# A third batch's best keys searched at the end of the causal attention, and the local attention's second half of the first norm on ScalarE

## The chip, the cores and the metric

The program runs on one core of a Trainium2 chip. The metric is the device time of one execution of the whole program in microseconds (us). A kernel stands with the median of its runs. Beside them one execution was taken by the hardware profiler; all times of engines below are from it, counted from the start of its span. In its views PE is TensorE, PEld its weight loads, DVE VectorE, ACT ScalarE, POOL GpSimd, SP SyncE, which issues the transfers.

## The reference, cut to what matters

Twelve layers follow each other, each `x = x + layer(norm(x))`, with x of 8 batches of 128 tokens and 128 features. The change touches three layers in a row.

- `L1_attn`, causal attention with 16 heads of width 64: softmax(q k / scale) v, projected.
- `L1_xattn`, attention to a context in which each query keeps only its 32 best keys: 4 heads of width 32; per row of 128 scores the 32 largest are kept, the rest is left out of the softmax. Its probabilities, averaged over the heads, weigh the context's values; a product with `film` gives scales and shifts (FiLM) for the layer's inputs, which are x normed twice, times `g_norm_in` plus `b_norm_in`. A long convolution along the tokens (a state space model) and a two-layer MLP follow.
- `L1_ffn`, two small blocks, each a local attention with l2-normed, rotated queries and keys (8 heads of width 64) and a gated MLP.

## The kernel before, in words

Every layer is one or two blocks. In a block each engine has a list of instructions of its own, run in order; semaphores (`wait_ge`, `then_inc`) tie the lists, and at a block's end all engines meet. Next to nothing is planned at run time: the order is the order of the loops.

**Causal attention (`layer_l1_attn`).** The loop runs over turns -6 to 16; turn n holds step n of 16 (half a batch, 8 heads), and in it TensorE turns the probabilities of step n (L2339), makes the scores of step n+2 (L2375, L2379) and the value products of step n (L2395); ScalarE takes the exponentials of step n+1 (L2463) and copies step n's result (L2490); VectorE copies turned probabilities (L2556), inverts sums (L2561) and takes maxima of step n+2 (L2602); GpSimd divides the probabilities of step n+1 (L2253). In turns 4, 8, 14 and 16 two finished batches are projected (L2353) and GpSimd adds them to x (L2267). In between, work of the next layer is fitted in: the keys, queries and scores of batches 0 and 1, and `ROUNDS` says in which turn how many rounds of `BestKeys.one_round` VectorE runs. A round takes the eight largest of each row (`max`, L2122) and takes them out (`match_replace`, L2129) for four heads; four rounds make a batch. In turn 14 x's batches 2 and 3 are measured for the norm, in turn 16 they are normed (L2526), turned (L2303), copied, and their queries made (L2401); in turns 15 and 16 the keys of batches 2 to 7 are made (L2297); the scores of batch 2 close TensorE's list (L4023, L4026).

**Best keys (`top_attention`), called the top stage below.** VectorE finishes the norm's statistics and searches batches 2 to 7, four rounds each, with the norm of batches 4 to 7 (`dve_xn`, L464) after the second round. ScalarE copies scores out (L4251), takes the exponentials of a batch's scores (L4240, `exps`) and of what the search left (L4230, `exps_left`), and empties the banks of means (L4257), context (L4261) and FiLM (L4219, L4221). GpSimd subtracts the two (L4115), makes the weight from the two sums (L4104 to L4106) and multiplies (L4118, which marks `kept`), later modulates the inputs (L4123, L4127) and adds x to the shifts (L4130). In its turn 3 it begins the inputs of all 8 batches (L4096 to L4099). TensorE turns the kept probabilities (L4184), multiplies with the values (L4193) and with `film` (L4197, L4201), and makes the scores of a batch two turns on. `keep_clock_bf` (L134) gives it products that nobody reads: 8 before the loop, 6 and 5 near its end, 4 behind it. SyncE first issues the next layer's weights (3698 KB, L4776), then stores the convolution's taps to DRAM (L4071), waits for them and reads them back as rows (8 transfers of 1024 KB, L4077) for the next block, `state_space_out`, whose convolution (L4358) needs all of them.

**Local attention (`layer_l1_ffn`).** GpSimd takes the root of the second half's variance (L482, `norm.pool(pool, 1)`), makes tables (L3334), rotates (L3345, L3347) and takes powers (L3378). VectorE norms batches 4 to 7 (`norm.dve_xn(dve, 1)`, L464, four instructions), then sums squares of batch 2 (L3769), which ScalarE has squared (L3601). TensorE turns the normed batches (L488); the copies of them (L3594 by ScalarE, L3701 by VectorE) stand before the first value products (L3500).

## Time and the profile before

| | us |
|---|---|
| median of 3 runs (lowest, highest) | 1181.59 (1180.98, 1185.31) |
| the profiled execution, its own time | 1178.47 |
| its span, first to last instruction | 1176.7 |
| top stage, from its first instruction on VectorE to the first product of the convolution | 362.23 to 421.55 |

Over the whole span TensorE is busy 91%, VectorE 57%, ScalarE 47%, GpSimd 39%; these are means over stages with different limits. In a timeline a row gives the start, the duration, the engine, the line and operation, and in brackets how long the engine stood idle before it and which instruction ended that. The granted TensorE clock is given as a share of 2.4 GHz: 0.50 is its lower level, 1.2 GHz.

### The profile page before, as it was taken

How to read it: one execution, taken by the hardware profiler on the slowest of the kernel's cores; microseconds unless marked ns; L12 is line 12 of the kernel's file. 1: busy time of each engine (PE TensorE's matmuls, PEld its weight loads, DVE VectorE, ACT ScalarE, POOL GpSimd, SP SyncE). 2: the span in 40 equal slices, each digit the busy share in tenths (PEclk: the TensorE clock that was granted, in tenths of full speed). 3: DMA queues.
4: the chain of work that ended last, by engine and by line, in shares of the span. 5: the costliest groups of instructions: out<-in, count | busy, mean ns of one | idle time of the engine just before them, and what ended most of it. 6: DMA issues, size and time to landing. Idle time of an engine off the chain costs nothing. (4 is left out here: it accounts for less than half of the span.)

```text
span 1176.7 us, 22941 instructions
## 1 busy us (share of the span) xinstructions
PE 1065.6 (91%) x8781; PEld 765.7 (65%) x8797; DVE 673.5 (57%) x2055; ACT 557.6 (47%) x1473; POOL 461.4 (39%) x545
## 2 busy tenths in 40 slices
PE   6999989899997689898999899978899999988996
PEld 5876858567674355676677566745567776666684
DVE  5555562445767846885678467638823117766512
ACT  5434334266575844355445455506543334653432
POOL 7968913123245943783487250012000004041423
PEclk9999999899998799999999999999999999999999
DMA  5000060232205801000000030000021100010312
GB/s 168 1 1 5 2 232 1 94 105 73 73 2 205 216 2 46 1 1 1 1 2 1 1 76 2 2 5 33 1 81 36 36 19 17 2 41 2 130 48 77
DMA packets 55084, 54.18 MB, mean 46 GB/s; under 512 B 19472, under 2 KB 45840, under 8 KB 53952
## 3 DMA queue, kind: packets, MB, share of 16 engines
q1 hardware_dynamic: 54048, 50.84, 14.0%
q0 software_dynamic: 928, 1.88, 0.5%
q8 instruction: 71, 1.16, 0.4%
q14 instruction: 37, 0.30, 0.1%
HBM read 44.08 MB, written 8.63 MB: 45 GB/s over the span
## 5 line engine op out<-in xcount | busy, mean ns | idle before, releaser
L482 POOL TENSOR_TENSOR ln_rstd<-ln_ve,ln_half 128x4 f32<-128x4 f32 x25 | 25.4, 1018 | 251.7 <-DVE ln_ve L457 251.7
L652 DVE TENSOR_REDUCE scratch<-bank 128x4 f32<-128x512 f32 x96 | 63.3, 684 | 31.2 <-PE bank L557 18.1
L1311 ACT ACTIVATE scratch<-bank 128x512 f32<-128x512 f32 x64 | 38.2, 596 | 66.2 <-PE bank L1267 66.2
L713 ACT ACTIVATE scratch<-bank 128x512 f32<-128x512 f32 x96 | 55.5, 597 | 23.4 <-PE bank L572 23.0
L2253 POOL TENSOR_TENSOR scratch<-scratch 128x512 f32<-128x512 f32 x32 | 33.3, 1040 | 82.7 <-DVE scratch L2561 82.6
L1330 DVE SCALAR_TENSOR_TENSOR x_res<-bank,scratch,x_res 128x128 f32<-128x128 f32 x64 | 18.0, 344 | 82.1 <-PE bank L1277 82.1
L1277 PEld LDWEIGHTS bank<-weights,scratch 128*128 128x128 f32 x512 | 59.5, 192 | 7.2 <-issue 7.2
L572 PE MATMUL bank<-ident,scratch 128*128 128x128 f32 x384 | 56.8, 278 | 7.9 <-ACT scratch L707 6.0
L3378 POOL TENSOR_TENSOR scratch<-scratch 128x16 f32<-128x16 f32 x16 | 50.6, 3163 | 33.4 <-DVE scratch L3774 24.9
L1267 PE MATMUL bank<-xnT,weights 128*128 128x512 f32 x128 | 59.2, 606 | 0.7 <-ACT xnT L1300 0.7
L1277 PE MATMUL bank<-weights,scratch 128*128 128x128 f32 x512 | 59.6, 275 | 0.0
L572 PEld LDWEIGHTS bank<-ident,scratch 128*128 128x128 f32 x384 | 42.6, 141 | 20.3 <-ACT scratch L707 8.4
L659 DVE TENSOR_TENSOR scratch<-bank,scratch 128x512 f32<-128x512 f32 x72 | 47.2, 683 | 0.8
L2463 ACT ACTIVATE scratch<-bank,scratch 128x128 f32<-128x128 f32 x128 | 45.0, 386 | 4.1 <-DVE scratch L2602 4.0
L3994 POOL TENSOR_TENSOR scratch<-scratch 128x1024 f32<-128x1024 f32 (+5 forms) x48 | 42.9, 894 | 3.8
L3989 POOL TENSOR_TENSOR scratch<-scratch 128x2048 f32<-128x2048 f32 x8 | 36.2, 4524 | 17.3 <-DVE weights L1870 16.9
L1267 PEld LDWEIGHTS bank<-xnT,weights 128*128 128x128 f32 x128 | 23.7, 196 | 24.7 <-issue 23.8
L1595 ACT ACTIVATE scratch<-bank 128x512 f32<-128x512 f32 (+1 forms) x44 | 22.7, 524 | 34.9 <-PE bank L1507 33.6
L3601 ACT ACTIVATE scratch<-bank 128x512 f32<-128x512 f32 x32 | 19.2, 599 | 40.4 <-PE bank L3415 40.4
L3036 POOL TENSOR_TENSOR scratch<-weights,xnT 128x128 f32<-128x128 f32 x8 | 3.4, 428 | 84.9 <-DVE weights L3252 84.9
L134 PE MATMUL bank<-key_bias,ident_bf 128*128 128x512 bf16 x115 | 33.9, 412 | 2.4 <-ACT weights L4275 1.1
L3415 PE MATMUL bank<-weights,xnT 128*128 128x512 f32 x64 | 31.8, 616 | 3.5 <-DVE scratch L3707 1.6
(645 smaller groups left out, 2913.7 us busy)
## 6 DMA issues: line engine op xcount, KB each, us to landing
scratch<-conv_kernels SPq DMA_DIRECT2D x8, 1024.0 KB, 11.2
weights<-e_l_ffn_w SPq DMA_DIRECT2D x20, 256.0 KB, 2.9
scratch<-e_l_ffn_w SPq DMA_DIRECT2D x4, 1024.0 KB, 15.2
values<-scratch SPq DMA_DIRECT2D x8, 512.0 KB, 2.7
scratch<-values SPq DMA_DIRECT2D x8, 512.0 KB, 4.3
weights<-w_l_ffn SPq DMA_DIRECT2D x1, 3698.0 KB, 11.6
scratch<-e_l_ffn_w SPq DMA_DIRECT2D x4, 768.0 KB, 6.9
weights<-w_l_attn SPq DMA_DIRECT2D x1, 2560.5 KB, 9.2
```

What stands on the lines that cost most here:

```text
L134: self.nc.tensor.matmul(self.ps[bank][:, :], self.ident_bf[:, :], self.key_bias[:, 0:BANK], start=True, stop=True)
L572: t = self.nc.tensor.transpose(self.core.ps[4 + n % 2][:, i * P:(i + 1) * P], self.shift[:, n % 4, i * P:(i + 1) * P], self.core.ident[:, :])
L652: self.nc.vector.tensor_reduce(self.top[:, n % 4, :], self.by_head(self.core.ps[n % 4][:, :]), AX_X, ALU.max, negate=True).then_inc(self.t ...
L659: self.nc.vector.tensor_tensor(self.by_head(self.shift[:, n % 4, :]), self.by_head(self.core.ps[n % 4][:, :]), self.top[:, n % 4, :].unsqu ...
L713: self.nc.scalar.activation(self.prob_of(n), self.by_head(self.core.ps[4 + n % 2][:, :]), ACT.Exp, scale=scale) \
L1267: nc.tensor.matmul(ps[UP_BANKS[i]][:, :], wa[e % 2][:, i * P:(i + 1) * P], core.xnT[:, half(h)], start=True, stop=True).then_inc(up_made.s ...
L1277: mm = nc.tensor.matmul(ps[Y_BANKS[u % 3]][:, t * P:(t + 1) * P], hT[h][:, i, t * P:(t + 1) * P], wb[e % 2][:, i, :], start=(i == 0), stop ...
L1311: nc.scalar.activation(hT[u % 2][:, i, :], ps[UP_BANKS[i]][:, :], act_func) \
L2463: a = nc.scalar.activation(prob[:, r, 4 * i + j, :], score_bank(n + 1, i)[:, j * P:(j + 1) * P], ACT.Exp, bias=top[:, r, 4 * i + j:4 * i + ...
L3378: nc.gpsimd.tensor_tensor(rn_first[:, s + 2, :] if s + 2 < FIRST else rn, ss, power, ALU.pow) \
L3989: link(tt(prod, z, wa[:, a].unsqueeze(1).broadcast_to([P, R, 2 * N]), ALU.mult))
L3994: link(tt(out, prod[:, :, 0:h], prod[:, :, h:2 * h], ALU.add))
```

## The change

It does six things.

1. Batches 2 and 3 of x are measured in turn 9, rooted and normed in turn 10, turned and copied in turn 11; their keys are made in turn 12 and their queries in turn 13. TensorE's products for it go to the bank of the step before, and VectorE, not ScalarE, empties them.
2. In turn 15 the scores of batch 2 (`score_third`) take the place of the keys' product; they lie in two banks and ScalarE copies them out. VectorE searches batch 2 in turn 16, four rounds (`STEPS: (4,)`). The scores of batch 3 close TensorE's list. ScalarE takes both exponentials of batch 0 in turn 16.
3. The inputs' first half (batches 0 to 3) is begun by GpSimd in turn 15 (`begin_inputs(..., 0)`), the second half in turn 3 of the top stage.
4. The top stage searches batches 3 to 7; the norm of batches 4 to 7 follows the first round; scores are made three turns ahead. Of the products nobody reads, the 8 before the loop and the 5 before the last batch's turning go, and 6 become 3.
5. The taps are stored at the end of SyncE's list in the causal attention. In the top stage SyncE reads the rows first and issues the next layer's weights behind them.
6. In the local attention GpSimd makes the offsets -mean times root (`pool_centred`), and ScalarE norms batches 4 to 7 with them (`act_xn`) in front of squaring batch 2; VectorE's four instructions go.

```diff
+    def pool_centred(self, pool, h, offset, centred):
+        core, nc, rows = self.core, self.nc, slice(B // 2 * h, B // 2 * (h + 1))
+        pool.wait_ge(self.eps.sem, self.half(self.eps, h))
+        nc.gpsimd.tensor_scalar(offset, core.ln_mv[:, rows, 0], -1.0, None, ALU.mult).then_inc(centred.sem, centred.up())
+        self.pool(pool, h)
+        pool.wait_ge(self.rstd.sem, self.half(self.rstd, h))
+        pool.wait_ge(centred.sem, centred.at(0))
+        nc.gpsimd.tensor_tensor(offset, offset, core.ln_rstd[:, rows], ALU.mult).then_inc(centred.sem, centred.up())
+
+    def act_xn(self, act, h, offset, centred):
+        act.wait_ge(centred.sem, centred.at(1))
+        for b in range(B // 2 * h, B // 2 * (h + 1)):
+            n = b - B // 2 * h
+            self.nc.scalar.activation(self.out[:, b, :], self.src[:, b, :], ACT.Identity, bias=offset[:, n:n + 1],
+                                      scale=self.core.ln_rstd[:, b:b + 1]).then_inc(self.xn.sem, self.xn.up())
...
+def begin_inputs(core, link, pool, search, u, g_in, b_in, h):
+    rows = slice(B // 2 * h, B // 2 * (h + 1))
...
+    link(tt(var, core.ln_mv[:, rows, 1], core.ln_rstd[:, rows], ALU.mult))
+    link(tt(var, var, core.ln_rstd[:, rows], ALU.mult))
+    link(ts(var, var, 1e-5, None, ALU.add))
+    link(tt(rstd, var, core.ln_half[:, rows], ALU.pow))
+    link(tt(part, core.xn[:, rows, :], rstd.unsqueeze(2).broadcast_to([P, B // 2, D]), ALU.mult))
+    link(tt(part, part, every(g_in), ALU.mult))
+    link(tt(part, part, every(b_in), ALU.add))
...
-    ROUNDS = {6: (0, 0, 0, 1), 7: (0, 0, 2, 0), 8: (2, 0, 1, 0), STEPS - 2: (0, 0, 2, 0)}
+    ROUNDS = {6: (0, 0, 0, 1), 7: (0, 0, 2, 0), 8: (2, 0, 1, 0), STEPS - 2: (0, 0, 2, 0),
+              STEPS: (4,)}
...
+            sp.dma_start(core.conv_dram.ap(), core.conv_kp).then_inc(taps.sem, taps.up(16))
+            sp.wait_ge(taps.sem, taps.at(0, 16))
...
+                if n == STEPS - 1:
+                    pool.wait_ge(*core.w_loaded["l1_xattn"])
+                    pool.wait_ge(ahead.rstd.sem, ahead.half(ahead.rstd, 0))
+                    pool.wait_ge(ahead.xn.sem, ahead.batch(ahead.xn, 3))
+                    pool.wait_ge(filled.sem, filled.at(place["yT", 2, 1]))
+                    begin_inputs(core, link, pool, search, inputs_at, g_in, b_in, 0)
...
+            def prepare_second_pair(n, out):
+                if n == 11:
+                    turn_rows(out, 2).then_inc(ahead.turned.sem, ahead.turned.up())
+                if n == 12:
+                    next_keys(0, out)
+                if n == 13:
+                    pe.wait_ge(x_out.sem, x_out.at(2))
+                    nc.tensor.matmul(out[:, 0:2 * P], wq_next, core.xnT[:, 2 * P:4 * P], start=True, stop=True) \
+                        .then_inc(queries_made.sem, queries_made.up())
...
                 if n == STEPS - 1:
-                    next_keys(0)
+                    pe.wait_ge(keys_out.sem, keys_out.at(0))
+                    pe.wait_ge(queries_out.sem, queries_out.at(0))
+                    score_third()
                 if n == STEPS:
-                    next_keys(1)
-                    pe.wait_ge(copied.sem, copied.at(2 * STEPS - 1))
-                    turn_rows(ps[T_BANKS[0]], 2).then_inc(ahead.turned.sem, ahead.turned.up())
+                    pe.wait_ge(third_copied.sem, third_copied.at(0))
+                    next_keys(1, ps[S_BANKS[1]])
+                if n in (11, 12, 13):
+                    pe.wait_ge(outs.sem, outs.at(n - 1))
+                    prepare_second_pair(n, ps[O_BANKS[(n - 1) % 2]])
...
             for t in range(1, B + 2):
-                if t == FIRST + 1:
-                    begin_inputs()
+                if t == 1:
+                    norm.pool(pool, 1)
+                if t == 3:
+                    norm.wait_xn(pool, B - 1)
+                    pool.wait_ge(norm.rstd.sem, norm.half(norm.rstd, 1))
+                    begin_inputs(core, link, pool, search, u, g_in, b_in, 1)
...
-            core.keep_clock_bf(QUERY_BANK, 8)
+            score(4)
...
-                if b == LAST:
-                    core.keep_clock_bf(SCORE_BANKS[3], 5)
...
-                    core.keep_clock_bf(SCORE_BANKS[3], 6)
+                    core.keep_clock_bf(SCORE_BANKS[3], 3)
...
+            core.load_following(sp)
...
-                        norm.pool(pool, 1)
+                        norm.pool_centred(pool, 1, norm_offset, norm_centred)
...
+                    if s == 0 and d == 0:
+                        norm.act_xn(act, 1, norm_offset, norm_centred)
                     if s + 2 < B:
                         square(g + 2)
...
                     if s == 0 and d == 0:
-                        norm.dve_xn(dve, 1)
                         sum_squares(g + 2)
```

## Rows read from the trace of the kernel before

**Rows 1.** The page: its first line, the span.

```profile
span 1176.7 us, 22941 instructions
```

**Rows 2.** Timeline: start, us, engine, line, operation, [idle before <-releaser]. A causal turn.

```profile
341.50 0.66 PE L2339 MATMUL bank<-ident,scratch 128*128 128x128 f32 x4 [0.51 <-POOL scratch L2253]
...
344.75 0.58 ACT L2490 COPY scratch<-bank 128x512 f32<-128x512 f32 x1 [0.91 <-PE bank L2395]
```

**Rows 3.** Timeline, last two turns of the causal attention and the stage change.

```profile
351.75 0.60 PE L2297 MATMUL bank<-ctxT_sb,weights 96*128 96x256 f32 x2
...
355.28 0.38 PE L2303 MATMUL bank<-ident,xn 128*128 128x128 f32 x2
...
359.37 0.70 PE L2401 MATMUL bank<-xnT,weights 128*128 128x256 f32 x2
...
359.47 0.62 ACT L2474 ACTIVATE scratch<-bank,weights 128x128 f32<-128x128 f32 x2 [3.13 <-PE bank L2353]
...
361.07 0.72 POOL L2267 TENSOR_TENSOR x_res<-x_res,scratch 128x256 f32<-128x256 f32 x1 [8.03 <-ACT scratch L2497]
...
362.23 0.49 DVE L444 BATCH_NORM_STATS2 ln_st<-x_res 128x6 f32<-128x128 f32 x2 [7.94 <-PEq L2226]
```

**Rows 4.** VectorE in the top stage: the norm, two starts of a search.

```profile
366.75 1.11 DVE L464 TENSOR_SCALAR xn<-x_res,ln_mv,ln_rstd 128x128 f32<-128x128 f32 x4
...
386.22 0.86 DVE L2122 MAX8 scratch<-weights 128x8 f32<-128x128 f32 x4
...
393.54 0.86 DVE L2122 MAX8 scratch<-weights 128x8 f32<-128x128 f32 x4
```

**Rows 5.** Groups in 362 to 422: xcount | busy us, mean ns | idle.

```profile
L4240 ACT ACTIVATE scratch<-weights 128x128 f32<-128x128 f32 x32 | 12.4, 394 | 0.0
```

**Rows 6.** Timeline of GpSimd in the top stage.

```profile
377.93 1.04 POOL L4096 TENSOR_TENSOR scratch<-xn,scratch 128x512 f32<-128x512 f32 x1
...
384.84 1.27 POOL L4115 TENSOR_TENSOR scratch<-scratch 128x512 f32<-128x512 f32 x1
...
387.47 0.27 POOL L4106 TENSOR_SCALAR scratch<-scratch,text_on 128x4 f32<-128x4 f32 x1
...
388.82 0.46 POOL L4123 TENSOR_TENSOR scratch<-scratch,weights 128x128 f32<-128x128 f32 x1
...
390.24 1.27 POOL L4115 TENSOR_TENSOR scratch<-scratch 128x512 f32<-128x512 f32 x1
...
410.66 0.46 POOL L4123 TENSOR_TENSOR scratch<-scratch,weights 128x128 f32<-128x128 f32 x1
```

**Rows 7.** TensorE, the top stage's last batches and the next stage.

```profile
401.49 0.80 PE L4193 MATMUL bank<-scratch 128*128 128x128 f32 x2 [0.36 <-ACT scratch L4257]
403.18 2.08 PE L4197 MATMUL bank<-weights,scratch 128*128 128x512 f32 x2 [0.90 <-ACT scratch L4261]
...
414.34 2.34 PE L134 MATMUL bank<-key_bias,ident_bf 128*128 128x512 bf16 x5
...
421.55 1.95 PE L4358 MATMUL bank<-scratch 128*8 128x128 f32 x64 [1.19 <-PEq L4067]
...
434.49 0.38 DVE L4475 TENSOR_TENSOR scratch<-bank,scratch 128x128 f32<-128x128 f32 x1
```

**Rows 8.** A stretch: us, busy time by engine, PEclk, DMA share, GB/s.

```profile
402.00:406.00 4.00, 3.10 (x8) 1.25 (x7) 4.00 (x28) 3.88 (x19) 3.60 (x7) 0.50 0.65 164
```

**Rows 9.** Timeline of SyncE's queue at the start of the top stage.

```profile
374.15 24.66 SPq L4077 DMA_DIRECT2D scratch<-conv_kernels  x8
```

**Rows 10.** Timeline at the first batches of the local attention.

```profile
471.35 1.01 POOL L482 TENSOR_TENSOR ln_rstd<-ln_ve,ln_half 128x4 f32<-128x4 f32 x1 [0.55 <-DVE ln_ve L457]
...
479.55 2.90 POOL L3378 TENSOR_TENSOR scratch<-scratch 128x16 f32<-128x16 f32 x1 [1.75 <-DVE scratch L3774]
...
474.77 3.37 DVE L464 TENSOR_SCALAR scratch<-x_res,ln_mv,ln_rstd 128x128 f32<-128x128 f32 x4
...
480.49 1.87 PE L3500 MATMUL bank<-scratch 128*128 128x65 f32 x12 [1.97 <-DVE xnT L3701]
```

## What the change should do to the time

> **What bounds the kernel now.** I read the page's first line for the size of the whole [rows 1] and then the timelines of the three stages that the change touches, since a mean over 1176.7 us says nothing of them. In each the question is which wait ends last.
>
> In the causal attention's late turns the work of a step goes from engine to engine in a ring: GpSimd divides, TensorE turns, VectorE copies, TensorE multiplies, ScalarE copies out and takes the next exponentials. TensorE waits for GpSimd (0.51 us) and ScalarE for TensorE (0.91 us) in the same turn [rows 2]: no engine is full, the ring itself is the limit, and what is put into it may lengthen it. At the stage's end the picture is another one. VectorE has nothing from 354.29 to 362.23 (7.94 us), ScalarE stands still for 3.13 us before the last projection arrives, and GpSimd's last addition, at 361.07, ends the stage [rows 3].
>
> In the top stage VectorE is never idle: a batch's search takes 393.54 - 386.22 = 7.32 us, and it does six [rows 4]. That looks like the bound, but it is not what ends the stage. GpSimd begins the inputs at 377.93 and takes batch 2 only at 384.84, 6.91 us later; from then on it takes one batch every 5.40 us with hardly a gap, up to the sixth's kept probabilities at 410.66 [rows 6]. TensorE's film product for that batch waits for them, five unread products follow at 414.34 (2.34 us), then the last batch, and the convolution starts at 421.55 [rows 7]. GpSimd's list ends last, the search a little before it.
>
> In the local attention four norm instructions take VectorE 3.37 us [rows 10], 0.84 each, where four of the same shape take 1.11 in all in the top stage [rows 4]; the sum of squares, GpSimd's power at 479.55 (1.75 us idle) and TensorE's value products at 480.49 (1.97 us idle) wait behind them [rows 10].
>
> **Causal attention, turns 9 to 14.** TensorE gets 0.38 (turning two batches), 0.60 (keys) and 0.70 us (queries) [rows 3], 1.68 us in turns 11 to 13, all of it between the turning and the value products, so in the ring. VectorE gets a norm of two batches (half of 1.11, 0.56 us [rows 4]), statistics (at most the same again) and three copies out of banks of 256 columns (0.38 to 0.60 each by the nearest rows [rows 3], 1.5 us at 0.5): 2.6 us. The copies of VectorE fall where TensorE is still busy with scores, and half of TensorE's extra falls into the waits for GpSimd (0.51 every second turn). Taken along the ring turn by turn, about 1.0 us stays. Bounds: 0 if the waits take all, 1.68 + 2.6 = 4.3 if nothing hides. The new waits of TensorE (for a step's copy out by ScalarE) come after the turning (341.50 in the turn shown [rows 2]), when the copy of the step before is past; behind them stand the scores, for which VectorE and ScalarE wait.
>
> **Causal attention, the end.** The search of batch 2 is 7.32 us of VectorE. Its cover is the idle 7.94 us plus the 0.56 of norm that leaves turn 16: 8.5 us, and the scores have to be there in time; they are, for they come where the keys' product stood (351.75) [rows 3] and VectorE is free only at about 353.7. So VectorE ends at about 361, beside GpSimd's last addition. Cost 0, margin about 1 us; without the cover, 7.3. ScalarE's eight exponentials, 394 ns each [rows 5], are 3.15 us in an idle time of 3.13 [rows 3]; the 256-column copy that leaves makes room. GpSimd's first half of the inputs (3.46 of big instructions, some 1.8 of small ones) lies in its 8.03 us of idleness [rows 3]. The turning (0.38) and part of the queries' product (0.70) leave the chain to the end: -0.4. The taps' transfer stands last in SyncE's list, behind transfers that are long done. Causal attention in all: +0.6, bounds -0.4 and +3.9.
>
> **Top stage.** VectorE loses one search of six, 7.32 us. GpSimd: batch 0's exponentials are ready, so it starts right after the root, at about 364.1, and is done 3.98 later (388.82 - 384.84 [rows 6]). Batch 1 needs its second exponentials, behind the copy of the turned norm; the norm now comes one round (1.83) earlier: 0.8 statistics, 1.83, 1.11 norm [rows 4], 1.1 turning, 0.6 copy and 4 x 0.394 [rows 5] after 362.2 give 369.2. Then 3.98 for batch 1, 1.8 for small instructions (four, nearest rows 0.27 and 1.01 [rows 6, 10]) and 6.91/2 = 3.46 for half the inputs: batch 2 starts at 378.5, not 384.84 [rows 6]. From there the pace is the old 5.40, since each batch costs what it cost: **-6.3 us**. The search does not hold it up: five searches and the norm end at 401, and the last batch's exponentials of what is left, at 404, come before GpSimd's last kept probabilities (410.66 - 6.3 = 404.4).
>
> The five unread products (2.34 us [rows 7]) stood between the sixth batch's film product and the last batch's turning; about 0.2 of it lay beside other work: **-2.1 us**. The eight and the three others stood in waits: 0. So -8.4 at an unchanged clock.
>
> The clock is not unchanged. From 402 to 406 it was granted at 0.50, the lower level [rows 8], though TensorE was busy 3.10 of 4 us; the film product took 2.08 us there and the values' product 0.80 [rows 7]. It is at 2.4 GHz when the convolution starts: 64 products in 1.95 us [rows 7]. Ahead of that stood the five unread products. With 16 such products gone the last two batches' products can take twice what they take at the higher level (half of 2.08, of 0.80 and of a turning like the latter, 1.9 a batch), +3.8, and the convolution's first 64 another 1.95: between 0 and +5.7. I take +2.0, since part of the last batches ran at the lower level before, too.
>
> The Trainium skill, "TensorE: Matmul & The Clock Gate", Part 1, says that the default state is throttled and that activity releases the throttle; that speaks against taking unread products out. The trace agrees as far as a lower level stands in the stretch with gaps. By it, in full, the stage would give the 5.7 and end near -2.7; by the rows of unread products alone it would be -8.4.
>
> The transfers: the eight row reads are issued from 374.15 on, over 24.66 us [rows 9], and the queues are still busy in part of 402 to 406 [rows 8], so they end near 404. They now start near 362.6 and end near 393; the next weights follow and are needed only behind 458. Cost 0; the rows would matter only if they came after 413. In all -6.4, bounds -8.4 and -2.7.
>
> **Local attention.** VectorE loses 3.37 us. GpSimd gets two small instructions (0.27 at most each [rows 6]) and two waits: its tables and rotation come 0.9 later. ScalarE gets four instructions of some 0.4 us (394 ns [rows 5]), 1.6 us, in front of squaring batch 2, which is late by as much; the power on GpSimd then starts at 478.65, when the rotation is over, not 479.55: -0.9. The normed batches are turned and copied at about 478.0, so the value products start 2.4 us before 480.49 [rows 10]. Which of the two counts? The next powers wait for TensorE's chain, with more idle time than 0.9 in front of them, so -2.2; bounds -0.9 and -2.5.
>
> **Sum.** +0.6 - 6.4 - 2.2 = -8.0. The profiled execution took 1178.47 (span 1176.7 [rows 1], 1.8 around it); it would become 1170.5. The median of the runs shown is 1181.59, 3.1 above it, so I predict 1173.6.
>
> **Rivals.** (a) The ring is lengthened by everything that is put in: +3.9 in place of +0.6, so -4.7, 1176.9. For it: no engine in it has slack in every turn [rows 2]; against: the waits of 0.51 and 0.91. (b) The clock stays low through the last batches and the convolution's start, +5.7 in place of +2.0: -4.3, 1177.3. (c) The clock does not fall: -10.0, 1171.6. (d) Slower: TensorE stays at 1.2 GHz through the whole convolution. That stage is 12.9 us (421.55 to 434.49 [rows 7]) and ordered by TensorE; doubled it adds 12.9, with 3.8 for the two batches 16.7 in place of 2.0: +6.7, 1188.3. It decides from 8.0 us of clock loss beyond my 2.0. Against it: the convolution is dense, 64 products in 1.95 us. (e) The change doesn't do what it says: the third search is not hidden but ends the stage. If the scores come late or the rounds slow down beside GpSimd, up to 7.3 - 1.0 = 6.3 of the gain is handed back: -1.7, 1179.9. Against it is the 8.5 us of cover [rows 3].
>
> **Chances.** Forecast, with all its terms near their values: 0.50. (a) 0.14, (b) 0.12, (c) 0.12, (d) 0.06, (e) 0.06. Half a per cent, 5.9 us, is about what a measurement can tell. The forecast's own range, 1171 to 1176, is beyond it in nine parts of ten: 0.45; with (c) and what of (a) and (b) ends beyond it, 0.63 faster; 0.30 the same; 0.07 slower. The range runs from the sum of the good bounds, -0.4 - 8.4 - 2.5 = -11.3, 1170.3 (1169.5 with a little for the median), to (e), 1180.
>
> **What would show it.** Right: VectorE searching up to the end of the causal attention and that stage no more than 2 us longer; GpSimd taking batch 2 some 16 us after the top stage's start and then every 5.4 us; the convolution starting 53 us after the stage's start, not 59.3; the four norms on ScalarE at about 0.4 us, value products about 2 us sooner. Wrong: a PE clock near 0.5 in the convolution; an idle VectorE in the top stage, waiting for scores of batch 4; a top stage in which ScalarE, not GpSimd, ends last; turns 10 to 13 more than 0.5 us longer each.

## The result: faster by 1.0%, more than forecast

| | before | after |
|---|---|---|
| median (lowest, highest), us | 1181.28 (1179.90, 1185.31) | 1169.22 (1168.38, 1170.57) |
| the profiled execution, us | 1178.47 | 1170.57 |
| its span, us | 1176.7 | 1168.8 |

The ratio is 0.990, with a 95% interval of 0.988 to 0.992, which is 10.0 to 14.4 us less. Forecast was 1173.6 with a range of 1169.5 to 1180.0: the direction was right, the gain a third too small, and the measured median 0.3 us below the range. Two later series of the same two kernels gave ratios of 0.991 (0.989 to 0.994) and 0.990 (0.988 to 0.991), so 10 to 12 us is the size to explain, and that the first median lies 0.3 us below the range is within what the series differ by.

Where it is, by stages of the two profiled executions (starts by SyncE's first transfer of a stage or VectorE's first statistics, ends by the next stage's start; the top stage ends with the convolution's first product):

| stage | before | after | difference | forecast |
|---|---|---|---|---|
| stage ahead of the causal attention (unchanged code) | 63.07 | 66.01 | +2.9 | 0 |
| causal attention | 142.64 | 143.27 | +0.6 | +0.6 |
| top stage | 59.32 | 51.34 | -8.0 | -6.4 |
| convolution and MLP | 36.56 | 36.57 | 0 | 0 |
| local attention | 221.58 | 218.42 | -3.2 | -2.2 |
| all behind it | 491.81 | 492.14 | +0.3 | 0 |

The three changed stages give -10.5 us. The +2.9 in unchanged code is no effect of the change: the same stage took 63.07 us in two other executions of changed kernels (again_2 and norm_back below) and 65.7 to 66.1 in most others. It goes with the granted clock, whose mean over this stage was 0.97 in the execution of before, 0.92 in that of after, 0.93 in "again" (65.77 us) and 1.00 in both_early (62.83 us).

The top stage after, GpSimd's timeline (start, duration, engine, line and operation, and in brackets how long the engine was idle and what ended that). These answer to [rows 6]; the subtraction is L4204 now, the modulation L4212:

```profile
381.76 1.10 POOL L4204 TENSOR_TENSOR scratch<-weights,scratch 128x512 f32<-128x512 f32 x1
...
387.00 1.27 POOL L4204 TENSOR_TENSOR scratch<-scratch 128x512 f32<-128x512 f32 x1
...
406.98 0.47 POOL L4212 TENSOR_TENSOR scratch<-scratch,weights 128x128 f32<-128x128 f32 x1
```

The reader is to see the starts of the large subtractions. The stage starts at 365.56; batch 2 (381.76) is taken 16.2 us later, where the forecast had 16.3 and the kernel before 22.6, and from there the starts are 5.24, 5.42, 5.33 and 5.42 apart. The kept probabilities of batch 6, the last that GpSimd makes (the prediction calls it the sixth), are done at 407.0, 41.5 us after the start instead of 48.5. The durations of L4204 alternate between 1.09 or 1.10 and 1.27; before, all seven took 1.27.

TensorE at the end of the stage, answering to [rows 7]:

```profile
408.93 1.81 PE L4281 MATMUL bank<-weights,scratch 128*128 128x512 f32 x2 [0.35 <-ACT scratch L4345]
...
410.96 1.06 PE L4268 MATMUL bank<-ident,scratch 128*128 128x128 f32 x4
...
416.90 1.95 PE L4441 MATMUL bank<-scratch 128*8 128x128 f32 x64 [1.57 <-PEq L4168]
```

and the granted clock there (a stretch, its length, TensorE's busy time and instructions, PEclk, DMA share, GB/s), answering to [rows 8]:

```profile
404.00:408.00 4.00, 2.17 (x7) 1.00 0.06 24
...
410.00:412.00 2.00, 2.00 (x7) 0.50 0.00 0
...
414.00:418.00 4.00, 2.43 (x48) 1.00 0.01 2
```

From 404 to 408 the clock is 1.00, from 410 to 412 it is 0.50, and the film product (1.81 us) and the turning (1.06) are drawn out there; ahead of the convolution it is back at 1.00. From 404 on the transfers have all but ended (24 GB/s), and TensorE waits for none.

The causal attention's end, answering to [rows 3]:

```profile
357.19 0.85 DVE L2156 MAX8 scratch<-weights 128x8 f32<-128x128 f32 x4
...
365.60 0.49 DVE L444 BATCH_NORM_STATS2 ln_st<-x_res 128x6 f32<-128x128 f32 x2 [1.01 <-PEq L2265]
...
364.43 0.73 POOL L2315 TENSOR_TENSOR x_res<-x_res,scratch 128x256 f32<-128x256 f32 x1 [3.18 <-ACT scratch L2580]
```

VectorE searches from 357.19 to 364.6 where it stood idle for 7.94 us; the next stage's statistics come 1.01 us after that, and GpSimd's last addition ends at 365.16, 0.6 us after the search. The search is hidden.

The turns with the extra work, before and after: ScalarE copies out the results of steps 10, 11 and 12 (the first step is 0):

```profile
332.28 0.58 ACT L2490 COPY scratch<-bank 128x512 f32<-128x512 f32 x1 [0.18 <-PE bank L2395]
...
336.73 0.58 ACT L2490 COPY scratch<-bank 128x512 f32<-128x512 f32 x1 [0.91 <-PE bank L2395]
...
340.45 0.58 ACT L2490 COPY scratch<-bank 128x512 f32<-128x512 f32 x1 [0.33 <-PE bank L2395]
```

```profile
335.09 0.59 ACT L2573 COPY scratch<-bank 128x512 f32<-128x512 f32 x1 [0.17 <-PE bank L2476]
...
339.79 0.59 ACT L2573 COPY scratch<-bank 128x512 f32<-128x512 f32 x1 [1.14 <-PE bank L2476]
...
343.95 0.59 ACT L2573 COPY scratch<-bank 128x512 f32<-128x512 f32 x1 [0.77 <-PE bank L2476]
```

They were 4.45 and 3.72 us apart and are 4.70 and 4.16: 0.69 us more, and every other distance between the copies is the old one within 0.02 us. From the last copy to the next stage it takes 7.62 us instead of 7.80.

The local attention, answering to [rows 10]:

```profile
468.30 1.65 ACT L482 ACTIVATE scratch<-x_res,scratch,ln_rstd 128x128 f32<-128x128 f32 x4 [5.15 <-POOL scratch L476]
...
473.66 1.97 PE L3601 MATMUL bank<-scratch 128*128 128x65 f32 x16 [1.36 <-DVE xnT L3804]
475.47 1.04 PE L3532 MATMUL bank<-ident,scratch 128*128 128x128 f32 x8
```

The four norms take ScalarE 0.41 us each. The value products start 20.2 us after the stage's start (453.47), before 22.4 (480.49 - 458.11): 2.2 sooner. They and the turning behind them take 1.97 and 1.04 us; before, they took 2.72 and 1.91, with the clock at its lower level. The row in [rows 10] gives 1.87 us and 12 products because its view ended at 482; all 16 are here:

```profile
480.49 2.72 PE L3500 MATMUL bank<-scratch 128*128 128x65 f32 x16 [1.97 <-DVE xnT L3701]
483.01 1.91 PE L3431 MATMUL bank<-ident,scratch 128*128 128x128 f32 x8
```

```profile
482.00:484.00 2.00, 2.00 (x11) 2.00 (x11) 1.51 (x5) 0.00 (x0) 1.20 (x2) 0.50 0.00 0
```

In this last view of before each engine has a busy time, TensorE first; the granted clock is the third number from the end. GpSimd's power starts 20.2 us after the stage's start, before 21.4: 1.3 sooner (forecast 0.9).

### The profile page after: what moved, and what is told of

Same layout as the page of the kernel before. It is cut to its first block and busy times, and to the rows that moved or that the text cites. A ratio compares the mean times of both kernels' runs of the same rounds, so it can differ in the third digit from the quotient of the medians.

```text
span 1168.8 us, 22936 instructions
## 1 busy us (share of the span) xinstructions
PE 1063.2 (91%) x8781; PEld 762.9 (65%) x8781; DVE 671.9 (57%) x2054; ACT 559.2 (48%) x1475; POOL 463.3 (40%) x551
## 3 DMA queue, kind: packets, MB, share of 16 engines
q0 software_dynamic: 928, 1.88, 0.5%
## 5 line engine op out<-in xcount | busy, mean ns | idle before, releaser
L2338 PE MATMUL bank<-xnT,weights 128*64 128x128 f32 x512 | 32.4, 277 | 2.6 <-DVE scratch L2660 1.0
## 6 DMA issues: line engine op xcount, KB each, us to landing
weights<-w_l_ffn SPq DMA_DIRECT2D x1, 3698.0 KB, 16.2
```

## Experiments

All kernels start from the changed one unless it says otherwise. The series ran on more than one chip (the kernel before took 1181 us in two of them and 1188 to 1190 in the others); a ratio is always to the kernel before of the same series, and stage lengths come from the profiled execution of each. "Kept" is the end of batch 6's kept probabilities, the last that GpSimd makes, counted from the stage's start.

| kernel | ratio (95% interval) | causal | kept | top stage | local |
|---|---|---|---|---|---|
| before | 1 | 142.64 | 48.5 | 59.32 | 221.58 |
| after, first | 0.990 (0.988, 0.992) | 143.27 | 41.5 | 51.34 | 218.42 |
| again | 0.991 (0.989, 0.994) | 142.79 | 41.5 | 50.69 | 218.40 |
| again_2 | 0.990 (0.988, 0.991) | 143.10 | 41.4 | 51.27 | 218.38 |
| norm_back | 0.994 (0.992, 0.996) | 143.10 | 41.4 | 51.30 | 221.28 |
| norm_keep | 0.990 (0.989, 0.992) | 141.79 | 42.9 | 52.07 | 219.90 |
| norm_alone (from before) | 0.999 (0.997, 1.000) | 142.49 | 48.5 | 58.97 | 218.59 |
| five_back | 0.991 (0.989, 0.993) | 142.84 | 41.5 | 51.26 | 218.39 |
| keepers_all | 0.994 (0.992, 0.996) | 142.66 | 44.2 | 55.45 | 218.36 |
| e_placed | 0.990 (0.988, 0.992) | 143.14 | 41.2 | 51.53 | 218.38 |
| halves_late | 0.995 (0.994, 0.997) | 142.81 | 47.0 | 56.25 | 219.14 |
| rounds_four | one run | 142.98 | 48.1 | 57.59 | 218.38 |
| rounds_late | one run | 142.74 | 42.8 | 56.76 | 219.16 |
| norm_later | one run | 142.65 | 44.4 | 54.30 | 218.36 |
| end_more | one run | 142.78 | 42.9 | 52.48 | 218.56 |
| no_adds | one run | 142.71 | 40.5 | 50.30 | 218.39 |
| left_first | 0.992 (0.991, 0.994) | 143.22 | 43.5 | 52.91 | 218.38 |
| left_placed | 0.992 (0.990, 0.993) | 142.90 | 43.6 | 52.81 | 219.15 |
| mean_early | 0.991 (0.989, 0.993) | 142.71 | 42.5 | 51.69 | 219.14 |
| both_early | 0.990 (0.988, 0.992) | 141.69 | 42.2 | 51.45 | 218.39 |

**The change again (again, again_2).**

> The changed kernel once more. The three changed stages of its first profile sum to 10.5 us less than before (0.7 more in the causal attention, 8.0 less in the top stage, 3.2 less in the local attention). If that is the whole change, five rounds give 10.0 to 11.2 us below the kernel before; if the first medians' difference of 12.1 us is real, something outside these stages gives 1.5 us.

> The changed kernel on this chip, for comparison with the two below, and a third measurement of the change itself: 10.0 to 11.2 us below before if the three stages are all of it; 12 if the first measurement's median was right.

The kernel was 10.6 and 11.8 us below before. The three changed stages account for 10.0 to 11.7, by three executions of the changed kernel and two with the old code in the first two stages (before, and norm_alone). Nothing outside them is needed, and nothing outside them is seen; 10.6 is what was expected of the three stages alone, and the 11.8 of again_2 lies between its two values, 10.0 to 11.2 and 12.

**The local attention's edit undone (norm_back).**

> The changed kernel with the local attention's norm as before: VectorE norms batches 4 to 7, GpSimd makes no offsets. By the prediction's term the kernel is 2.2 us slower than the changed one and its value products keep TensorE's full clock. By the rival, a fall of the clock after TensorE's idle time of about 2 us costs another 1.0: 3.2 us slower, with a slice at 0.50 and value products of 2.7 us instead of 2.0 in this stage.

```diff
-                        norm.pool_centred(pool, 1, norm_offset, norm_centred)
+                        norm.pool(pool, 1)
...
-                    if s == 0 and d == 0:
-                        norm.act_xn(act, 1, norm_offset, norm_centred)
...
                     if s == 0 and d == 0:
+                        norm.dve_xn(dve, 1)
                         sum_squares(g + 2)
```

The median is 3.1 us above the same chip's "again", the stage 2.9 longer. TensorE of this kernel and its granted clock:

```profile
472.91 2.07 PE L3601 MATMUL bank<-scratch 128*128 128x65 f32 x16 [1.94 <-DVE xnT L3802]
474.78 1.91 PE L3532 MATMUL bank<-ident,scratch 128*128 128x128 f32 x8
```

```profile
474.56:476.56 2.00, 2.00 (x12) 0.52 0.00 0
```

TensorE is idle for 1.94 us, starts its value products 22.35 us after the stage's start, and the clock falls behind that, to 0.52 and in the next slice 0.63: the turning takes 1.91 us where after it takes 1.04. So here the edit is worth 3 us, not 2.2, and a fall of the clock follows the idle time. The edit makes the fall rarer and does not rule it out: in 4 of the 17 executions with the edit the clock fell at this place all the same (halves_late, rounds_late, left_placed, mean_early). The idle time ahead is 1.34 to 1.38 us in all 17, and the local attention of the four took 219.14 to 219.16 us instead of 218.4 to 218.6. One slice of halves_late, 22 us into the stage:

```profile
478.50:480.50 2.00, 2.00 (x11) 0.51 0.00 0
```

**The idle time filled (norm_keep).**

> The changed kernel with the local attention's norm as before (VectorE norms batches 4 to 7) and seven products that nobody reads between the turning of the normed batches and the first value products, where TensorE stood idle for 1.94 us. If the edit's gain of 3.0 us was 2.0 to 2.2 from the earlier start and about 1.0 from a clock that did not fall, the local attention takes about 220.3 us here (221.3 without the seven products, 218.4 in the changed kernel) and the value products take 1.04 us instead of 2.07. If the clock has no part in it, it stays at 221.3.

```diff
                         turn_x(d, 1)
+                        core.keep_clock_bf(O_BANKS[0], 7)
```

```profile
474.63 1.97 PE L3601 MATMUL bank<-scratch 128*128 128x65 f32 x16
476.44 1.04 PE L3532 MATMUL bank<-ident,scratch 128*128 128x128 f32 x8
```

```profile
474.43:476.43 2.00, 1.97 (x17) 1.00 0.00 0
```

The value products start at the same place (22.2 us after the stage's start), the clock stays at 1.00, the turning takes 1.04 and the stage 219.90 instead of 221.28. So of the edit's 2.9 us, 1.4 are the clock that doesn't fall and 1.5 the earlier start, when the fall is taken away first. Taken the other way, between executions that both show the fall (norm_back and halves_late, 221.28 and 219.14), the earlier start is worth 2.1 and the fall 0.8. One number of the expectation missed: the value products themselves took 1.97 against 2.07, not 1.04; it is the products behind them that doubled. The medians of norm_back and norm_keep lie further apart (0.994 and 0.990) than the stage explains, and no other stage shows the rest. Norm_keep's top stage, with the code of the changed kernel, took 52.07 us and its kept probabilities came at 42.9: the granted clock was at its lower level from about a microsecond after the stage's start (see end_more below).

**That edit alone, on the kernel before (norm_alone).**

> The kernel before with the local attention's edit alone (offsets by GpSimd, the second half of the norm by ScalarE). If the edit's worth doesn't hang on the rest: about 3.0 us faster than before, its local attention 218.4 us long. By the prediction's term: 2.2. Its top stage is that of before, taken a second time: 59.3 us there, or up to 1.8 us off if the length of that stage changes with where the granted clock falls, as it did between executions of the changed kernel (50.7 to 52.5).

The diff is that of the change's sixth point. The stage is 218.59, 3.0 us shorter, as expected; its clock did not fall behind the idle time. The median of ten runs is only 1.3 us lower, with an interval from 3.8 us lower to 0.4 higher: the runs were spread over 7 us, and this comparison does not tell 3 us from 1. The trace decides here, not the median.

**The five products put back (five_back), and all of them (keepers_all).**

> The changed kernel with five products that nobody reads put back before the last batch's turning. If they stand on the path at the low clock and keep nothing up, as the prediction took them: 2.1 us slower. If their removal was what kept the low stretch so late and short: between 0 and 1 us slower, with the slices after 408 at a higher clock. If they hide in TensorE's wait for the last kept probabilities: no change.

> The changed kernel with all the products that nobody reads put back in the top stage: 8 ahead of the loop, 6 instead of 3, and 5. If they hold the clock up, the slices of the stage at 0.50 are fewer and the stage is 50.5 us or less. If they are only on the path, as the prediction took five of them: 2 us or more longer, 53.4. If the clock falls with them as without, and they lie in TensorE's waits: 51.0 to 51.9.

```diff
                 open_film(b)
+                if b == LAST:
+                    core.keep_clock_bf(SCORE_BANKS[3], 5)
```

and for keepers_all besides 8 behind `score(4)` and 6 in place of 3. With five_back the median stays (0.5 us below "again", the interval of either is wider). Its tail against that of "again", in which the clock was 1.00 behind 404 as in five_back:

```profile
406.47 0.66 PE L4270 MATMUL bank<-ident,scratch 128*128 128x128 f32 x4 [0.56 <-POOL scratch L4207]
...
409.79 1.24 PE L134 MATMUL bank<-key_bias,ident_bf 128*128 128x512 bf16 x5
...
416.22 1.95 PE L4443 MATMUL bank<-scratch 128*8 128x128 f32 x64 [1.57 <-PEq L4168]
```

```profile
405.42 0.66 PE L4268 MATMUL bank<-ident,scratch 128*128 128x128 f32 x4 [0.48 <-POOL scratch L4207]
...
408.74 0.60 PE L4268 MATMUL bank<-ident,scratch 128*128 128x128 f32 x4
410.17 0.49 PE L4277 MATMUL bank<-scratch 128*128 128x128 f32 x2 [0.83 <-ACT scratch L4341]
...
414.58 1.95 PE L4441 MATMUL bank<-scratch 128*8 128x128 f32 x64 [1.57 <-PEq L4168]
...
408.47 1.28 ACT L140 ACT_TABLE_LOAD   x1
...
409.87 0.25 ACT L4341 COPY scratch<-bank 128x128 f32<-128x128 f32 x1
```

In five_back the five take 1.24 us, not 2.34, and the convolution starts 9.75 us after the turning of batch 6, in "again" 9.16: 0.6 us for all five. The second of its expectations holds for the stage. The reason is in ScalarE's line: between two batches it loads a table (1.28 us) and copies the turned probabilities only at 409.87, so TensorE, done with turning at 409.3, waits 0.83 us for it. Taking the five away moved the wait from TensorE's list to ScalarE's. keepers_all tells the rest, and its stage of 55.45 us lies above all that was expected of it: the eight ahead of the loop (seven of them in the trace) took 3.19 us (the clock was falling) and stood in front of the first batch's turning:

```profile
372.10 3.19 PE L134 MATMUL bank<-key_bias,ident_bf 128*128 128x512 bf16 x7 [0.33 <-issue]
...
376.40 0.27 ACT L4344 COPY scratch<-bank 128x128 f32<-128x128 f32 x1 [3.98 <-PE bank L4271]
```

ScalarE stood idle 3.98 us, the kept probabilities came 2.8 us later and the stage took 4.1 to 4.8 us longer. That the eight could go was no side matter. No gain in clock stands against it. The first 20 us of the stage and the next 20, in keepers_all and in again_2 without the 16 products:

```profile
363.52:383.52 20.00, 14.88 (x81) 0.74 1.07 274
383.52:403.52 20.00, 14.54 (x48) 0.66 1.04 337
```

```profile
362.90:382.90 20.00, 13.75 (x77) 0.74 1.06 275
382.90:402.90 20.00, 14.68 (x50) 0.66 1.04 337
```

The granted clock is the third number from the end: 0.74 and 0.66 in both, and 0.74 and 0.67 in norm_alone, whose top stage is that of before. But the same code differs by more from one execution to the next: 0.53 and 0.62 in norm_keep, 0.57 and 0.66 in end_more, 0.73 and 0.59 in "again". So these means show no effect of the products and could not show a small one.

**What GpSimd has to do (halves_late, e_placed, no_adds).**

> The changed kernel with the first half of the inputs begun in the top stage too, right ahead of the second half. It puts 5.4 us more on GpSimd there and takes them from the causal attention's end. If GpSimd's chain sets the top stage, as the prediction took it: the stage is 5 us longer, 56.3 us, and the kernel 4.5 to 5.4 us slower. If VectorE's search sets it: no change. A gain of up to 0.5 at the causal attention's end would show that GpSimd's last addition stood on the path there.

```diff
-                    begin_inputs(core, link, pool, search, inputs_at, g_in, b_in, 0)
...
+                    begin_inputs(core, link, pool, search, u, g_in, b_in, 0)
                     begin_inputs(core, link, pool, search, u, g_in, b_in, 1)
```

The kept probabilities came 5.6 us later, the stage took 56.25, and the ratio is 0.4 to 0.6% worse than in the three series of the changed kernel (4.6 to 6.9 us, of which 0.7 is the local attention with its fallen clock). The forecast's bound by GpSimd holds on that side.

> The changed kernel with the second buffer of exponentials moved from the scratch buffer to the weights buffer (the modulation's two tiles change places with it, and the weights buffer is 64 columns longer). If the subtraction's time hangs on where its operands lie, all seven take 1.09 us instead of three taking 1.27, and if GpSimd's chain ends the stage, the stage is 0.5 us shorter. If the length comes from what VectorE does meanwhile, three go on taking 1.27 us and nothing changes.

```diff
-    e, e_left = [search.e0, c.take(H, P)], [search.e_left0, c.take(H, P)]
+    e, e_left = [search.e0, spare.take(H, P)], [search.e_left0, c.take(H, P)]
-    film_in = spare.take(2, P)
+    film_in = c.take(2, P)
-WEIGHTS = 7680
+WEIGHTS = 7744
```

The groups of the subtraction, after and in e_placed (output<-inputs, shapes, count, busy us and mean ns of one):

```profile
L4204 POOL TENSOR_TENSOR scratch<-weights,scratch 128x512 f32<-128x512 f32 x4 | 4.4, 1094 | 0.1
L4204 POOL TENSOR_TENSOR scratch<-scratch 128x512 f32<-128x512 f32 x3 | 3.8, 1267 | 0.8 <-ACT scratch L4314 0.8
```

```profile
L4204 POOL TENSOR_TENSOR scratch<-weights,scratch 128x512 f32<-128x512 f32 x7 | 7.6, 1090 | 1.2 <-ACT scratch L4314 0.8
```

The same instruction takes 1.09 us when its inputs lie in two buffers and 1.27 when both lie in one. The moved buffer took all of them to 1.09, and of 0.53 us less work ahead of the kept probabilities (three subtractions) 0.23 arrived. That was the hint that something lies right beneath GpSimd's chain. The stage, expected 0.5 us shorter, took 51.53, no less than after's. In this execution the clock stayed at 0.50 from 44 to 50 us after the start, and the four unread products behind the last batch took 1.65 us instead of 1.03:

```profile
414.77 1.65 PE L134 MATMUL bank<-key_bias,ident_bf 128*128 128x512 bf16 x4
```

They end at 416.42, 0.9 us after VectorE's last instruction of the stage (415.54), and the convolution follows them by 0.57. In after they end 0.65 us before VectorE's last (415.33 and 415.98). So at the lower level the unread products themselves end the stage here.

> The changed kernel in which GpSimd leaves out the addition of the normed x to the shifts (so the layer's output lacks it): 0.46 us less for each batch, four of them ahead of the last kept probabilities. If GpSimd's own work sets the rhythm: 4.95 us per batch, the last kept probabilities 1.8 us sooner, at 39.6 instead of 41.5. If a ring through TensorE and ScalarE lies right beneath: the rhythm stays at 5.2 to 5.4, GpSimd shows idle time ended by ScalarE's exponentials, and the kept probabilities come 0 to 0.6 us sooner.

```diff
-                    pool.wait_ge(film_out.sem, film_out.at(4 * b + 3))
-                    nc.gpsimd.tensor_tensor(shift_out[:, b, :], shift_out[:, b, :], core.xn[:, b, :], ALU.add)
```

This kernel leaves out x in the layer's output, so only its time means anything. Four batches' additions, 1.84 us, went, and the kept probabilities came 0.9 us sooner: between the two theories. GpSimd in that kernel:

```profile
384.88 1.27 POOL L4204 TENSOR_TENSOR scratch<-scratch 128x512 f32<-128x512 f32 x1 [0.32 <-ACT scratch L4312]
```

The first two waits, 0.32 and 0.37 us, are ended by ScalarE's exponentials; the starts (379.70, 384.88, 390.30, 395.12, 400.20) are 5.18 and 5.42 apart there and 4.82 and 5.08 later. What GpSimd waits for there is ScalarE's list. From 379.70 to 384.88 and from 384.88 to 390.30 ScalarE is busy 5.07 of 5.18 and 5.34 of 5.42 us and waits for nobody; it also copies out scores of later batches there. In the next two distances it is busy 4.45 of 4.82 and 4.71 of 5.08. So for these batches ScalarE's own work is as long as GpSimd's, and then it isn't. A ring (kept probabilities, TensorE's turning, ScalarE's copy and exponentials, GpSimd's next subtraction but one) is seen where ScalarE waits for TensorE's turning, 1.91 us at batch 1 and 0.60 at batch 4; in between ScalarE does not wait for it.

**The ring's start (left_first, left_placed, mean_early, both_early).**

> The changed kernel with ScalarE's exponentials of what the search left of batch 1 ahead of the copy of the turned batches, 1.7 us of work moved forward. GpSimd's second subtraction then starts as soon as GpSimd is free, at 5.9 instead of 6.7. If the chain from there is GpSimd's, the stage is 0.8 us shorter. If the copy, and with it the queries, the scores of batch 4 and TensorE's turning of batch 0 behind them, becomes late (by up to 1.5 us), the ring gives it back: 0, or up to 0.7 us longer.

> The changed kernel with left_first's order and e_placed's buffers. If both gains add: 1.0 us less until the last kept probabilities (0.8 and 0.2), and the kernel 1 us faster than the changed one; if the ring binds, no more than e_placed alone gave, 0.2.

> e_placed with TensorE turning the kept probabilities of batch 0 ahead of the queries and the scores of batch 4, and ScalarE copying the result out ahead of the queries. GpSimd's second subtraction stays at 6.7, but the ring starts 1 us sooner. If the ring took back part of the placement's gain: the last kept probabilities at 41.0 instead of 41.2. If turning waits for the first kept probabilities and holds up the queries: no gain, 41.2 to 41.6.

> mean_early with left_first's order: everything that the ring theory asks for. If the turning of batch 0 behind the queries was what made left_first slower, GpSimd's chain now keeps its 0.8: second subtraction at 5.9, last kept probabilities at 40.3 to 40.6 instead of 41.5, and the kernel 0.8 to 1.1 us faster than the changed one. If late queries and scores of batch 4 were the cause, they are late here too (by 2 us or more) and the kept probabilities come at 42 or later.

```diff
             exps(1)
+            exps_left(1)
             act.wait_ge(norm.turned.sem, norm.half(norm.turned, 1))
             nc.scalar.copy(core.xnT[:, half(1)], ps[TURN_BANK][:, :]).then_inc(x_out.sem, x_out.up())
-            exps_left(1)
```

and, for mean_early and both_early, on TensorE and ScalarE:

```diff
             norm.pe(pe, 1, TURN_BANK)
+            turn_kept(0)
             pe.wait_ge(x_out.sem, x_out.at(0))
...
+            take_mean(0)
             act.wait_ge(queries_made.sem, queries_made.at(0))
```

(`turn_kept(b)` is the loop's `open_film(b)`, its waits and its four transposes.) left_first, TensorE and GpSimd:

```profile
388.71 1.27 POOL L4204 TENSOR_TENSOR scratch<-scratch 128x512 f32<-128x512 f32 x1 [0.98 <-ACT scratch L4314]
...
371.98 2.07 PE L4253 MATMUL bank<-xnT,weights 128*128 128x512 f32 x2 [1.88 <-ACT xnT L4355]
...
376.00 1.06 PE L4268 MATMUL bank<-ident,scratch 128*128 128x128 f32 x4
```

GpSimd's second subtraction did start at 5.9 us (371.60), and the last kept probabilities came 2.1 us later all the same, the stage's end 1.6 to 2.2 later, more than either expectation allowed. TensorE waits 1.88 us for the copy that is now behind, turns batch 0 at 376.00, 10.3 us after the stage's start instead of 7.9 (after) or 8.6 ("again"), and GpSimd waits 0.48 and 0.98 us for ScalarE further on. left_placed adds the moved buffer to it and stays at 43.6. mean_early is no gain either: 42.5 where 41.0 to 41.6 was expected. With the turning of batch 0 ahead of the queries and left_first's order (both_early) the kept probabilities come at 42.2, not at the hoped for 40.3 to 40.6. But that execution had the lower level from a microsecond after the stage's start, as norm_keep had with the changed kernel's code, and against norm_keep (42.9, stage 52.07) it is 0.6 us shorter; its runs (1173.4 to 1181.0) enclose those of again_2 on the same chip. So for both_early it is not shown which of its two expectations holds, nor that it gains nothing. No version is measured to beat the changed kernel: the ratios of the four are 0.990 to 0.992, its own 0.990, 0.990 and 0.991. In left_first the wait of 0.79 us that looked free was not free: what was moved into it made TensorE's turning late.

**VectorE's cover (rounds_four, rounds_late, norm_later, end_more).**

> The changed kernel with 32 MAX8 whose results nobody reads ahead of VectorE's searches in the top stage, about 7 us, as much as the search of one batch: what the top stage would be if VectorE still had six batches to search beside the shorter GpSimd chain. VectorE is done with its last search 2.5 us before ScalarE needs it and its last product 1.1 us before TensorE does. If that is all the cover, the stage is about 3.4 us longer, near 54.7 us, and moving the third search is what made half of the stage's gain possible. If GpSimd alone sets it, it stays at 51.3.

> The changed kernel with 32 MAX8 whose results nobody reads behind the norm in VectorE's list in the top stage (about 7 us, the search of one batch), so that the norm isn't held up as it was with them in front. If VectorE's cover is small, as its last search ending 2.5 us before ScalarE needs it says, the last batch's product by VectorE ends near 49.3 and the stage takes 54.6 to 55.3 us. If GpSimd alone sets the stage: 51.3.

> The changed kernel with the norm of batches 4 to 7 behind the second round of the search, as before, instead of the first. If ScalarE's list hangs on it (the copy of the turned batches stands ahead of the exponentials that GpSimd's second subtraction needs), that subtraction starts 1.8 us later, at 8.5 instead of 6.7, and GpSimd's whole chain and the stage with it: 53.1 us. If GpSimd's start is set by its own work: 51.3.

> The changed kernel with 8 MAX8 whose results nobody reads behind the third batch's search in the causal attention's last turn, about 1.7 us. The search ends 1.0 us before the next stage's statistics start. If the search is hidden with that margin, the causal attention is 0.7 us longer, near 143.9; if it is what already ends the stage, 1.7 us, near 144.9; if the end hangs on TensorE alone, no change.

```diff
                     search.one_round(dve, t, r, free)
                     if t == FIRST and r == 0:
                         norm.dve_xn(dve, 1)
+                        for k in range(32):
+                            nc.vector.max(unread[:, k, :], core.ident[:, :])
```

is rounds_late; rounds_four has the 32 ahead of the loop, norm_later has `r == 1`, end_more 8 such behind the search in turn 16. rounds_four missed by 3 us, and it was the experiment that was wrong: in front of the loop they delay the norm, too, and GpSimd's second subtraction came at 12.9 instead of 6.7. Behind the norm (rounds_late) it stayed at 6.7, and the stage still took 56.76 us:

```profile
408.10 0.40 ACT L4314 ACTIVATE scratch<-scratch,weights 128x128 f32<-128x128 f32 x1 [1.97 <-DVE scratch L2163]
...
409.96 0.80 PE L4277 MATMUL bank<-scratch 128*128 128x128 f32 x2 [2.59 <-ACT scratch L4341]
```

ScalarE waits 1.97 us for VectorE's last rounds, and the copy of batch 6's turned probabilities stands behind those exponentials, so TensorE waits 2.59 us. The expectation had counted with the last batch alone and missed that queue; with a low clock in the last batches it makes 5.4 to 6.1 us, not 3.3 to 4.0. The cover over the search is small: a sixth search in the top stage would have cost most of what moving it gained. norm_later: the second subtraction at 9.25, 2.5 us later, the kept probabilities 3.0 later, the stage 3.0 to 3.6 longer, where 1.8 was expected; a round earlier for the norm is worth more than a round. end_more: from ScalarE's last copy of a result to the next stage it takes 8.54 us, 0.9 more than in seven other executions of this code (7.61 or 7.62), near the 0.7 that a margin of 1.0 gives. The stage's 142.78 doesn't show it, since the causal attention's length differs by as much between executions of the same code (141.7 to 143.3 in the table). That difference lies ahead of the first copied result, 34.6 to 36.1 us after the stage's start, where the clock was at 0.50 for the first 3 to 7 us; from the first result to the last it is 99.51 to 99.59 us in all of them. Its top stage, with the same code, took 1.1 to 1.8 us longer than in the three executions of the changed kernel. There TensorE's first products ran at the lower level. They also did so in norm_keep, the second row:

```profile
363.16 3.34 PE L4250 MATMUL bank<-weights,ctxT_sb 96*128 96x128 f32 x16 [2.19 <-PEq L2265]
```

```profile
363.83 2.67 PE L4247 MATMUL bank<-weights,ctxT_sb 96*128 96x128 f32 x16 [1.27 <-PEq L2265]
```

16 products took 3.34 us against 2.02 in "again", and everything that ScalarE copies was late by it: the kept probabilities came 1.4 us later. The idle time ahead was 2.19 us against 1.27, but it is not shown that this made the clock fall: in norm_keep it was 1.27 too, the products took 2.67, and the kept probabilities were 1.4 us late as well.

## Why the prediction was right in its sign and short in its size

The median fell by 4.1 us more than forecast. The three changed stages account for 2.5 of it: the top stage was 1.6 better (two steps failed, the clock's +2.0 and the five products' -2.1, and GpSimd's chain was 0.7 too small), the local attention 1.0 (its term left out the clock that fell before the change). The other 1.6 stand in no changed stage; the later series, 10.6 and 11.8 us, lie nearer to the stages.

- **Causal attention, +0.6:** right. The ring grew by 0.7 us where about 1.0 was forecast, and the end became 0.2 shorter where 0.4 was: +0.5. The whole stages, from two executions of before and three of after, give between +0.2 and +0.8. The third search is hidden, rival (e) is out, and most of what was put into the ring lies in waits: rival (a) would have shown +3.9. The "margin about 1 us" behind the search was 1.01.
- **GpSimd's chain, -6.3:** the mechanism was right to the tenth up to batch 2 (16.2 us after the stage's start, forecast 16.3). The step that failed is "from there the pace is the old 5.40, since each batch costs what it cost". Three of the five last subtractions cost 1.09, not 1.27, because the exponentials' first buffer had moved: 0.5 us. (In the kernel before, the distances were 5.40 but for one of 5.64, so "5.40" was a little short, too.) The chain measured -7.0 (48.5 to 41.5). norm_later, halves_late and keepers_all each undo or add one thing and give back 3.0, 5.6 and 2.8 us. Together that is more than 7.0; that in the kernel before these delays lay beside one another, behind GpSimd's 6.91 us for the inputs, would explain it and was not measured.
- **"The eight and the three others stood in waits: 0"**: wrong as a general statement. In the new order the eight would have been on the path (keepers_all). The sum didn't suffer, since it was made for a chain without them.
- **The five unread products, -2.1:** mis-sized. five_back against "again" gives 0.6 at the full clock. Their 2.34 us [rows 7] was the length at the lower level, and behind them stood a cover that the prediction didn't name: ScalarE's table load. Rows of another engine at the same time would have shown it.
- **The clock, +2.0:** the step that failed most. Behind the kept probabilities the clock fell once in the kernel before and once after, and by the same: 0.81, 0.50 and 0.84 in the slices of 2 us from 412 on before, and 0.81, 0.50 and 0.84 from 408 on after. The middle one of before, against 410 to 412 above:

```profile
414.00:416.00 2.00, 2.00 (x7) 0.82 (x6) 0.00 (x0) 1.29 (x2) 0.86 (x2) 0.50 0.00 0
```

So the removal cost no clock in this pair. From the kept probabilities to the convolution it took 10.9 us before (10.4 in norm_alone), 9.9 after, 9.2 in "again" with a clock of 1.00 throughout, and 10.3 in e_placed with 0.50 from 44 us on. In these executions the lower level costs at most 1.1 us there. With 0.6 for the five products, some -0.4 is left where +2.0 was forecast; what makes that -0.4 is not shown. The two errors, +1.5 and -2.4, nearly cancel: of the 1.6 us by which the stage beat the forecast they make 0.9, GpSimd's chain the other 0.7. The Trainium skill's rule ("TensorE: Matmul & The Clock Gate", Part 1: throttled by default, activity releases) was a reason to expect a loss from taking products out. The trace does not bear it out here: with the 16 products, without them and with them again (norm_alone, again_2, keepers_all) the mean granted clock of the stage's first 40 us was the same within 0.01, and executions of the same code differ by more. Where an idle time of 2 us was filled (norm_keep), the rule and the trace agree.
- **Rival (c), "the clock does not fall", -10.0, 1171.6:** the nearest of all. Nothing was lost to the clock. It gives the top stage -8.4 where -8.0 was measured, and with 1.0 more from the local attention it would be -11.0 in all, beside the measured -10.5. It had a chance of 0.12, and its number was inside the range. (b) and (d) are out: the convolution ran at 1.00 and took 36.57 us with its MLP as before. The first half of (b), a low clock through the last batches, did come in e_placed, and its stage of 51.53 us was 0.2 to 0.8 longer than the changed kernel's.
- **Local attention, -2.2:** mis-sized, 3.0 (three comparisons: 2.9, 3.0, 3.2). The earlier start of the value products was right (2.2 against a forecast of 2.4). What was missing is the clock on this side: behind TensorE's idle 1.97 us [rows 10] it fell in the kernel before, and with the shorter wait it stayed at 1.00 in 13 of 17 executions. norm_keep measured 1.4 for it and 1.5 for the start; in the four in which the clock fell in spite of the edit the gain is 2.1 to 2.4, the forecast's number. The prediction asked of the clock only whether the change would make it fall, never whether it would stop a fall.
- **The median:** 3.1 us were added to the profiled execution of before. Its stage ahead of the causal attention happened to be the short one (63.07), after's the long one (66.01), so the two profiled executions differ by 7.9 us and the medians by 12.1.

Four lengths that vary in unchanged code go with the granted clock of the execution: the stage ahead of the causal attention (see the first table), the causal attention's first 36 us, the convolution's stage (38.26 us in keepers_all and mean_early, where the clock went to 0.50 about 19 us into it, and 36.56 elsewhere, at 1.00), and the local attention (219.15 and 218.4, above). The same holds of the top stage: the executions of its changed code took 50.69, 51.27, 51.34 and, with the lower level almost from the start, 52.07 us, so the clock moves it by more than a microsecond whatever the code.

Not settled: where these low stretches fall, which differs between executions of one kernel; and why the change of blocks ahead of the convolution takes 0.37 us more after the change (TensorE idle 1.57 us against 1.19 [rows 7]).

## What to carry to other kernels

Where TensorE stands idle for a microsecond or two and then has a dense run, look at the slices of the granted clock behind the wait, in more than one execution: a change that shortens the wait may be paid twice, once in the start and once in the clock, but the second payment did not come every time. An instruction on the path is worth what the next list lets through, not what it lasts: before a product is priced at its duration, read what every other engine does in that moment (here a table load took over half of it). And when one engine sets a chain's pace, ask how full the next engine is and how long the ring over the others; here both were hardly shorter. Before the lengths of a stage in two executions are compared, compare their granted clocks: norm_keep's top stage has the changed kernel's code and took 0.7 to 1.4 us longer, with the lower level almost from its start.

## What the runs showed of the hardware

- GpSimd's subtraction of 128x512 fp32 takes 1.09 us with its two inputs in different buffers and 1.27 us with both in the same one; moving a buffer switched all seven to 1.09.
- After an idle time of 1.94 us in the local attention the granted clock went to 0.52, and 8 turnings took 1.91 instead of 1.04; with seven products in the gap it stayed at 1.00. With an idle time of 1.34 to 1.38 us it stayed at 1.00 in 13 executions and fell in 4, which cost 0.8 us of the stage.
- In the top stage 16 products more or less left the mean granted clock at 0.74 and 0.66; executions of the same code lay between 0.53 and 0.74 in its first 20 us.
- The same five products took 2.34 us in one execution and 1.24 in another, by the clock of the moment.
